# The top-1 stage of eight experts: dense over all tokens in two-part float32r, or routed by expert in places of 128 rows in plain float32

## The reference

```python
n = layernorm(h)                         # 1664 x 192
p = softmax(n @ Wg)                      # Wg: 192 x 8
e = argmax(p)                            # the token's expert
y = silu(n @ W1[e] + b1[e]) @ W2[e] + b2[e]   # 192 -> 768 -> 192
h = h + p[e] * y
```

## Time and profile before

| | |
|---|---|
| median of 3 executions | 3536.33 us (3533.74 to 3541.62) |
| profiled execution, its own time | 3540.45 us |
| its span, first to last instruction | 3538.6 us |
| mean granted TensorE clock | 0.925 of full |
| the two phases of the second layer's feed-forward | 2052.8 to 2464.9 us of the span |

### The profile page before, as it was taken

How to read it: one execution, slowest core, us unless ns; L and a number is a source line. 1 busy time by engine, 2 the same in 40 slices (tenths; PEclk the granted TensorE clock), 3 DMA queues, 4 the chain that set the end, 5 groups by cost and what they waited for, 6 DMA issues and landing times. The chain is left out here.

```text
span 3538.6 us, 61221 instructions
## 1 busy us (share of the span) xinstructions
PE 3168.4 (90%) x21505; PEld 2959.4 (84%) x21505; DVE 2348.5 (66%) x5839; ACT 1209.5 (34%) x2419; POOL 645.9 (18%) x733
## 2 busy tenths in 40 slices
PE   6769999999999999999699879999887879876687
PEld 6659999999999999999688869998676869865476
DVE  2656777777777777777486747777447657776666
ACT  2332333333333333333333333333435333234233
POOL 1111111111111111111211111111222211121220
PEclk8779999999999999999899979999998979988698
DMA  2010000000000000000000000000000010000000
GB/s 96 1 47 16 33 32 32 31 32 32 32 32 32 32 32 32 32 32 0 34 2 2 33 16 32 32 16 9 1 10 1 17 47 16 10 1 3 12 17 15
DMA packets 9707, 82.40 MB, mean 23 GB/s; under 512 B 1285, under 2 KB 1541, under 8 KB 3194
## 3 DMA queue, kind: packets, MB, share of 16 engines
q1 hardware_dynamic: 9466, 79.59, 6.1%
HBM read 78.29 MB, written 1.30 MB: 22 GB/s over the span
## 5 line engine op out<-in xcount | busy, mean ns | idle before, releaser
L716 ACT ACTIVATE hid<-bank,dat 128x384 f32<-128x384 f32 (+1 forms) x1104 | 671.7, 609 | 1404.6 <-PE bank L446 1272.6
L685 PE MATMUL bank<-w,hid_hi 128*128 128x384 f32 x3588 | 1038.2, 361 | 0.0
L687 PE MATMUL bank<-w,hid_lo 128*128 128x192 f32 x3588 | 901.8, 251 | 0.0
L687 PEld LDWEIGHTS bank<-w,hid_lo 128*128 128x128 f32 x3588 | 687.1, 191 | 1.9
L748 DVE TENSOR_TENSOR hid_lo<-hid,hid_hi 128x384 fp32r<-128x384 f32 (+1 forms) x1104 | 653.6, 592 | 38.4
L685 PEld LDWEIGHTS bank<-w,hid_hi 128*128 128x128 f32 x3588 | 674.0, 188 | 1.9
L745 DVE CAST hid_hi<-hid 128x384 fp32r<-128x384 f32 (+1 forms) x1104 | 413.0, 374 | 174.5 <-ACT hid L716 173.1
L759 DVE SCALAR_TENSOR_TENSOR h_tok<-bank,gate,h_tok 128x192 f32<-128x192 f32 x520 | 216.8, 417 | 318.6 <-PE bank L687 312.1
L446 PE MATMUL bank<-xa_hi,w_hi 128*128 128x384 f32 (+1 forms) x1104 | 402.2, 364 | 9.9 <-DVEq L1741 5.6
L446 PE MATMUL bank<-xa_hi,w_lo 128*128 128x384 f32 (+1 forms) x1104 | 394.3, 357 | 0.0
L446 PE MATMUL bank<-xa_lo,w_hi 128*128 128x384 f32 (+1 forms) x1104 | 394.1, 357 | 0.0
(11 more groups left out here) (291 smaller groups left out, 4234.1 us busy)
## 6 DMA issues: line engine op xcount, KB each, us to landing
raw<-in_L_exp SPq DMA_DIRECT2D x44, 1344.0 KB, 5.7
pix<-in_pixels SPq DMA_DIRECT2D x6, 832.0 KB, 9.1
wp_raw<-in_L_att SPq DMA_DIRECT2D x1, 2880.0 KB, 9.4
raw<-in_L_mlp SPq DMA_DIRECT2D x2, 1344.0 KB, 5.7
wp_raw<-in_L_att SPq DMA_DIRECT2D x2, 768.0 KB, 4.1
tok<-in_tok SPq DMA_DIRECT2D x1, 1248.0 KB
out<-h_tok SPq DMA_DIRECT2D x1, 1248.0 KB, 4.4
wp_raw<-in_L_fat SPq DMA_DIRECT2D x1, 960.0 KB, 4.8
```

The lines of the kernel that those rows point to most:

```text
L685: nc.tensor.matmul(o[:, 0:2 * D], hid_hi[k % 2][:, m, c], w2[j][:, m, :], start=m == 0, stop=False)
L687: ins = nc.tensor.matmul(o[:, 0:D], hid_lo[k % 2][:, m, c], w2[j][:, m, 0:D], start=False, stop=m == HC - 1)
L716: nc.scalar.activation(hid[(6 * k + m) % 3][:, 0:128 * nt], bank[4 + (6 * k + m) % 4][:, 0:128 * nt], func, bias=bias).then_inc(s["h_act"] ...
```

## The change

The two phases keep their place and are written anew. No float32r splits are left in them. `features_phase(plain=True)` evacuates the turned tokens in float32 (`x_f`) and leaves out VectorE's low parts, and no weights are split beside it. The logits are made token-major: 26 products, two for each tile, with the tile's turned tokens stationary and the 8 gate columns moving. `routed_phase` then sorts the tokens by expert: VectorE counts the chosen tokens over the tiles (`cum`), TensorE ranks them, VectorE works out a destination row for each token (`slot`) and the expert of each place (`place`). A place is 128 rows of one expert; there are always 20 of them (`PLACES`, (1664 + 8 x 127) // 128), whatever the routing. GpSimd scatters the 13 tiles of normalised tokens to a DRAM table `route_rows` by 13 indirect DMAs. Then for each place: SyncE reads the expert's number from `place`, loads that expert's weights (1,348 KB, three buffers `w_e`) and the place's 128 rows (`x_in`, four buffers); TensorE turns the rows (`turn`), VectorE copies them out of PSUM (`keep_x`), TensorE makes the six hidden chunks with two float32 products each (`up`), ScalarE applies Silu, TensorE makes the result with six products (`down`, one place later), VectorE copies it (`keep_y`) and GpSimd scatters it to a DRAM table `route_back` by token number. At the end SyncE reads the 1,664 rows back in four loads and VectorE adds them, scaled, to `h_tok`. A cleared table of 2 MB is written to `route_rows` at the start of the kernel.

```diff
+ROW = 200
+PLACES = (TOK + 8 * 127) // 128
+PACK = RAW + 8
+ROUTE_COLS_8 = 128 + 128 + 13 * 8 + 64 + PLACES * 8
...
-                        for o in ((feat[:, part, c],) if ln else ((xa_hi, xb)[part][:, c],)):
+                        for o in ((feat[:, part, c],) if ln else (x_f[:, part, c],) if plain else ((xa_hi, xb)[part][:, c],)):
...
-                for i, (t0, n) in enumerate(TBLK):
+                for i, (t0, n) in enumerate(() if plain else TBLK):
...
+                if plain:
+                    w = dat[:, DATA_COLS[g_col]].rearrange("p (k e) -> p k e", k=2)
+                    for t in range(TILES):
+                        c = slice(128 * t, 128 * t + 128)
+                        nc.tensor.matmul(bank[0][:, E * t:E * t + E], x_f[:, 0, c], w[:, 0, :], start=True, stop=False)
+                        ins = nc.tensor.matmul(bank[0][:, E * t:E * t + E], x_f[0:DB, 1, c], w[0:DB, 1, :], start=False,
+                                               stop=True)
+                    ins.then_inc(s["job_full"].sem, 1)
+                    return
...
+            def sync(sp):
+                sp.wait_ge(route["places"], 1)
+                for p in range(N):
+                    if p >= 3:
+                        sp.wait_ge(route["y_full"], p - 2)
+                    e = sp.value_load(place[0:1, p:p + 1], min_val=0, max_val=E - 1)
+                    sp.dma_start(w_e[p % 3][:, :], pack[bass.ds(e, 1)].rearrange("o p n -> p (o n)"))\
+                        .then_inc(w_e_in[p % 3], 16)
+                    if p == 0:
+                        sp.wait_ge(route["rows_out"], 16 * TILES)
+                    if p >= 4:
+                        sp.wait_ge(y_out[p % 4], 16 * (p // 4))
+                    sp.dma_start(x_in[p % 4][:, :], rows_d[128 * p:128 * p + 128, :]).then_inc(x_e_in[p % 4], 16)
+                for j in range(4):
+                    sp.wait_ge(y_out[j], 16 * (N // 4))
+                for q, (t0, nt) in enumerate(BLOCKS):
+                    sp.dma_start(y_tok[:, t0:t0 + nt, :], back_d[128 * t0:128 * (t0 + nt), :]
+                                 .rearrange("(t p) d -> p t d", p=128)).then_inc(y_tok_in[q], 16)
+
...
+            def gpsimd(pool):
+                pool.wait_ge(route["rows_clear"], 16)
+                pool.wait_ge(route["tables"], 32)
+                pool.wait_ge(route["slots"], 1)
+                for t in range(TILES):
+                    nc.gpsimd.indirect_dma_start(rows_d[:, :], bass.IndirectOffsetOnAxis(slot[:, t:t + 1], 0),
+                                                 x_ext[:, t, :], None).then_inc(route["rows_out"], 16)
+                for p in range(N):
+                    pool.wait_ge(route["y_kept"], p + 1)
+                    pool.wait_ge(x_e_in[p % 4], 16 * (p // 4 + 1))
+                    nc.gpsimd.indirect_dma_start(
+                        back_d[:, :], bass.IndirectOffsetOnAxis(x_in[p % 4][:, D:D + 1].bitcast(I32), 0),
+                        y_e[p % 4][:, :], None).then_inc(y_out[p % 4], 16)
+            def tensor(pe):
+                gating["tensor"][0](pe)
...
+                nc.tensor.matmul(bank[0][:, TILES * E:TILES * E + E], ones, last[:, TILES - 1, :], start=True, stop=True)
+                nc.tensor.matmul(o, tri, chosen, start=True, stop=False)
+                nc.tensor.matmul(o[:, E:], ones, last[:, 0:TILES - 1, :].rearrange("p t e -> p (t e)"),
+                                 start=False, stop=True).then_inc(route["ranked"], 1)
...
+                def turn(p):
+                    pe.wait_ge(x_e_in[p % 4], 16 * (p // 4 + 1))
+                    if p >= 2:
+                        pe.wait_ge(route["x_kept"], p - 1)
+                    ident = shp[:, SHAPE_COLS["ident"]]
+                    nc.tensor.transpose(bank[6 + p % 2][:, 0:128], x_in[p % 4][:, 0:DA], ident)
+                    nc.tensor.transpose(bank[6 + p % 2][0:DB, 128:256], x_in[p % 4][:, DA:D], ident)\
+                        .then_inc(route["x_turned"], 1)
+                def up(p):
+                    pe.wait_ge(w_e_in[p % 3], 16 * (p // 3 + 1))
+                    pe.wait_ge(route["x_kept"], p + 1)
+                    w = w_e[p % 3]
+                    for m in range(HC):
+                        n = HC * p + m
+                        if n >= 4:
+                            pe.wait_ge(route["hid_full"], n - 3)
+                        o = bank[n % 4][:, 0:128]
+                        nc.tensor.matmul(o, w[:, 128 * m:128 * m + 128], x_t[p % 2][:, 0:128], start=True, stop=False)
+                        nc.tensor.matmul(o, w[0:DB, HID + 128 * m:HID + 128 * m + 128], x_t[p % 2][0:DB, 128:256],
+                                         start=False, stop=True).then_inc(route["up_full"], 1)
+                def down(p):
+                    if p >= 2:
+                        pe.wait_ge(route["y_kept"], p - 1)
+                    for m in range(HC):
+                        pe.wait_ge(route["hid_full"], HC * p + m + 1)
+                        ins = nc.tensor.matmul(bank[4 + p % 2][:, 0:D], h_e[p % 2][:, m, :],
+                                               w_e[p % 3][:, 2 * HID + D * m:2 * HID + D * m + D],
+                                               start=m == 0, stop=m == HC - 1)
+                    ins.then_inc(route["y_full"], 1)
+                turn(0)
+                up(0)
+                for p in range(1, N):
+                    turn(p)
+                    up(p)
+                    down(p - 1)
+                down(N - 1)
...
+                steps = ((c3, cum[1], 1), (cum[1], cum[0], 2), (cum[0], cum[1], 4), (cum[1], cum[0], 8))
+                for f, o, w in steps:
+                    nc.vector.tensor_copy(o[:, 0:w, :], f[:, 0:w, :])
+                    link(nc.vector.tensor_tensor(o[:, w:TILES, :], f[:, w:TILES, :], f[:, 0:TILES - w, :], ALU.add))
...
+                def keep_x(p):
+                    dve.wait_ge(route["x_turned"], p + 1)
+                    if p >= 2:
+                        dve.wait_ge(route["up_full"], HC * (p - 1))
+                    nc.vector.tensor_copy(x_t[p % 2][:, 0:128], bank[6 + p % 2][:, 0:128])
+                    nc.vector.tensor_copy(x_t[p % 2][0:DB, 128:256], bank[6 + p % 2][0:DB, 128:256])\
+                        .then_inc(route["x_kept"], 1)
+                def keep_y(p):
+                    dve.wait_ge(route["y_full"], p + 1)
+                    if p >= 4:
+                        dve.wait_ge(y_out[p % 4], 16 * (p // 4))
+                    nc.vector.tensor_copy(y_e[p % 4][:, :], bank[4 + p % 2][:, 0:D]).then_inc(route["y_kept"], 1)
+                keep_x(0)
+                for p in range(1, N):
+                    keep_x(p)
+                    keep_y(p - 1)
+                keep_y(N - 1)
+                for q, (t0, nt) in enumerate(BLOCKS):
+                    dve.wait_ge(y_tok_in[q], 16)
+                    for t in range(t0, t0 + nt):
+                        nc.vector.scalar_tensor_tensor(res[:, t, :], y_tok[:, t, :], inv[:, t:t + 1], res[:, t, :],
+                                                       ALU.mult, ALU.add)
...
-        load, split, w = expert_weights(8, a["L1_exp"], ("av_full", signals["av_full"].at + 2 * 14))
-        attention(l1, h_tok, load)
-        features_phase(n_tok, split, norm_of=h_tok)
-        g = gates(8, "L1_g", None, "top1")
-        experts_phase(8, a["L1_exp"], "L1_b1", "L1_b2", h_tok, ACT.Silu, w, g)
+        attention(l1, h_tok)
+        features_phase(x_ext[:, :, 0:D], dict(sync=lambda sp, n=len(phases): sp.wait_ge(s["phase_done"].sem, 3 * n)), route_tables(), norm_of=h_tok, plain=True)
+        g = gates(8, "L1_g", None, "top1", plain=True)
+        routed_phase(a["L1_exp"], "L1_b2", h_tok, g)
...
+            sp.dma_start(route_rows, a["rows_clear"]).then_inc(route["rows_clear"], 16)
```

More of the change, by code:

```diff
@@ L191, in vit_tower @@
         at.close()
+        dp = ExitStack()
+        x_ext = sb("x_ext", [128, TILES, ROW], scope=dp)
+        x_f = sb("x_f", [128, 2, TOK], scope=dp)
+        rp = sb("rp", [128, ROUTE_COLS_8], scope=dp)
+        w_e = [sb(f"w_e{j}", [128, PACK], scope=dp) for j in range(3)]
+        x_in = [sb(f"x_in{j}", [128, ROW], scope=dp) for j in range(4)]
+        x_t = [sb(f"x_t{j}", [128, 256], scope=dp) for j in range(2)]
+        h_e = [sb(f"h_e{j}", [128, HC, 128], scope=dp) for j in range(2)]
+        y_e = [sb(f"y_e{j}", [128, D], scope=dp) for j in range(4)]
+        cum = [sb(f"cum{j}", [128, TILES, 8], scope=dp) for j in range(2)]
+        tot = sb("tot", [128, 8], scope=dp)
+        nbl = sb("nbl", [128, 3, 8], scope=dp)
+        wide = sb("wide", [128, 8 * PLACES], scope=dp)
+        slot_f = sb("slot_f", [128, TILES], scope=dp)
+        slot = sb("slot", [128, TILES], I32, dp)
+        place_f = sb("place_f", [1, PLACES], scope=dp)
+        place = sb("place", [1, PLACES], I32, dp)
+        dp.close()
         bank = [pb(f"bank{j}") for j in range(8)]
@@ L491, in exponents @@
                 NJ = TOK // 4
```

(28 more changed lines are left out.)

106 lines of the change are left out of this document (94 added, 12 removed).

## The result

The changed kernel takes **3373.06 us** (median of four runs, 3369.58 to 3377.08) against 3538.34 for the kernel before beside it: ratio 0.9534, 95% interval 0.9516 to 0.9552, 165 us less. The prediction was 208 us less, 3328; its range to 3390 holds the time, its likeliest case doesn't. The profiled execution's span is 3374.2 us.

What follows compares the result with a forecast made beforehand. It took TensorE's product work, with chains ahead, to bound the two phases. New terms 14.3 + 11.5 + 7.9 + 20.6 + 138 + 11.4 = 203.7 us replace 412.1, giving 3328 us; range 3295 to 3390.

Steps and rivals of the forecast that it cites:

- wrong if the period isn't paced by the load: Twenty places: a sign that would refute the forecast, which had a 6.7 us period paced by load and products together.
- What bounds the kernel, and the gain's direction: Replaced phases, 412.1 us: mostly TensorE's product work, with chains ahead; the change was to save 208.4 us, faster at 0.98.
- Features, 14.3: Features phase: 21.3 us falls by 7.0, without weight splits slowing two small VectorE operations and without low parts.
- Logits and gates, 11.5: Gates phase, 15.1 us before: 52 records make 8.0 us, VectorE's chain 3.3, getting into the phase 0.2.
- Sorting, 7.9: Sorting tokens by expert: VectorE's counts 2.0 us, TensorE 1.6, VectorE's chain of 13 to 14 operations 4.3.
- The end, 11.4: After the last place: `keep_y` 0.4 us, GpSimd 1.4, landing 2.4, four loads 5.5, last additions 1.7.
- Scatter, 20.6: Scatter of rows to `route_rows`: 13 indirect DMAs at 1.4 us, the geometric middle of 0.56 and 3.5, plus 2.4 landing.
- rival 4: Dear scatter: 3.5 us an issue, partly from VectorE's additions holding GpSimd up; 29 us more, 3357. Chance 0.14.
- The twenty places, 138: Loop over places: 14.1 us to the first `down`, 121.2 for 18 periods of about 6.7, last `down` 2.4.
- Up to 128 columns I use 0.112: Places: each record of `up`'s float32 products steps by 0.112 us, so its 24 records take 2.69 us.
- the phases behind are as they were: Phases after the new stage: no change of time; no term was given for them.
- Rival 3: Cold clock in the places: `up` and `down` at half clock, body 10.5 us, 76 us more, 3404. Chance 0.10.

Runs made afterwards that it cites:

- experiment 6: Changed kernel with its 64-row products kept, four weight buffers for three, ten buffers for rows and results for four: 3373.99 us, ratio 0.9539.
- Experiment 2: Changed kernel with the second logits product of each tile on all 128 rows, gate columns zero in rows 64 to 127: 3371.05 us, ratio 0.9528.
- experiment 1: Changed kernel with the second product of every hidden chunk in `up` on all 128 rows, the added rows zero: 3319.56 us, ratio 0.9373.
- experiment 7: Changed kernel with zero-filled 128-row second products in both `up` and the logits: 3317.55 us, ratio 0.9384.
- experiment 11: Changed kernel with 48 unused columns put back in table `dat`, so tiles behind it return to their old addresses: 3381.48 us, ratio 0.9552.
- experiment 3: Changed kernel with `up`'s chunks in pairs, two products of 128 rows, then the two of 64: 3347.31 us, ratio 0.9465.
- experiment 10: Rows loaded ahead of weights, on the changed kernel with 128-row products, four weight and ten row/result buffers, and `turn` between `up` and `down`: 3282.07 us, ratio 0.9275.

## Why the prediction was right or wrong, by its own steps

**The prediction's own sign**, "wrong if the period isn't paced by the load", came true: in the changed kernel TensorE's products pace every place, and the load is hidden (experiment 6). The time lies in the range, but the mechanism of the places failed.

**What bounds the kernel, and the gain's direction**: right. The dense experts were TensorE's work, and computing 20 x 128 rows for 8 x 1664 pays for everything added.

**Features, 14.3**: 13.2. The two small operations of the earlier trace rows are gone down to their short form, as the step said:

```profile
2046.46 0.17 DVE L432 TENSOR_SCALAR rstd<-mv 128x2 f32<-128x2 f32 x1
...
2047.99 0.17 DVE L432 TENSOR_SCALAR rstd<-mv 128x4 f32<-128x4 f32 x1
```

**Logits and gates, 11.5**: 14.5. The logits took 11.2 for 8.0; the row that I took (8 rows, all alike) had no change of rows in it. Experiment 2 gives 8.3.

**Sorting, 7.9**: 7.0. **The end, 11.4**: 10.7.

**Scatter, 20.6**: 18.6, from the sorted slots at 2080.3 to 2098.9, where the first place's rows are asked for; they are on the chip at 2100.9, 2.0 us that the prediction has in the places (2.4). The issue was cheaper than its term:

```profile
2082.63 0.96 POOL L869 DMA_INDIRECT route_rows<-x_ext,slot  x1 [0.30 <-issue]
2083.89 0.96 POOL L869 DMA_INDIRECT route_rows<-x_ext,slot  x1 [0.30 <-issue]
...
2090.21 0.96 POOL L869 DMA_INDIRECT route_rows<-x_ext,slot  x1 [0.30 <-issue]
2091.48 0.96 POOL L869 DMA_INDIRECT route_rows<-x_ext,slot  x1 [0.30 <-issue]
```

An issue steps by 1.26 us for the 1.4 of a geometric middle. The first begins 0.9 us behind the slots, thirteen take 16.3, and 1.4 after the last the rows are out. A geometric middle of two bounds six times apart was a guess, and that it came near was luck. The landing of these scatters, which the changed kernel's trace does not list, is 2.4 us in experiment 1's, as the term had it. The step is the same 1.26 while VectorE makes its additions (to 2086.2) and after them. So rival 4's hold did not occur.

**The twenty places, 138**: 192.3. This is the step that failed, and in it one sentence, "Up to 128 columns I use 0.112". The row is of products that all have 128 rows; `up`'s alternate. Per place at full clock that is 5.0 us for 2.69, and 8.07 for a body of 5.9. It makes the loads' 7.05 us hidden, and so the pacing that the step describes never began. Of the 54 us, (8.07 - 6.7) x 20 = 27 are this, (9.27 - 8.07) x 20 = 24 the clock, 0.83 over the places where I had chosen 0.9, and 3 remain. The cut is rough: the 6.7 already has a clock of 0.9 in it, and without that the first part is larger and the second smaller. In experiment 1, with equal rows, the clock is 0.94 (over its places) and the period 6.93. So most of the second half goes away with the first. What links them was not isolated.

The rest of the step held. `down`'s 0.178 was 0.171. The number's read costs less than the 1.0 us taken: `down(p-3)` ends near 2124.7, and the load that waits for it is issued at 2125.41. The rows are issued 0.38 us behind the weights and land 6.1 us later, so from `down(p-3)` to `turn(p)` the loads take 0.7 + 0.4 + 6.1 = 7.2 us for 7.05. The step's alternation, 6.4 and 7.1, shows in experiment 1 as 5.8 and 7.5 in the two places read there, and its period 6.7 was 6.75 in experiment 7, at a clock of 0.96 for the 0.9 taken; so near a hit has luck in it.

The Trainium skill (TensorE: Matmul & The Clock Gate, section on packing small matmuls) has the line that a weight load overlaps with a product in flight only when the row groups differ. This case's rows show the opposite of that line: next to a product on the same 128 rows the load begins 0.11 us ahead of its own product (experiment 1, 0.112 us a record), and where 128 and 64 rows alternate it begins only with it. The measurement decides.

**The sum.** The stage is 52.6 us above its term. Around it the time is 8.6 less: 7.2 ahead, nearly all of it experiment 11's addresses, and 1.4 behind. 3328 + 52.6 - 8.6 = 3372, measured 3373. The prediction had "the phases behind are as they were" and nothing on those ahead but the clearing, whose cost of nothing holds: it lands after 20.8 us, under the convolution, and the next loads are issued at 43.7 us for 44.9 before.

**The rivals.** Rival 3, the cold clock, was there in part: one place in three. (Its terms, 1.0 + 5.4 + 3.9, make a body of 10.3, not 10.5; that is 4 us in its total.) None of them, and not the range, had a longer product at full clock in it. The range held because it reached towards rival 3, for another reason: that the time lies in it is luck as far as the places go.

## What to carry to other kernels

Cost a product by a row whose neighbours are like its neighbours: a stream of like products tells nothing about a stream in which they alternate. Where a sum over 192 rows is cut in two, cut it in 96 and 96 (47 us here), fill the short part with zeros (54 us), or put products of like rows together (26 us). And when TensorE gets faster, look at the loads again: first the number of buffers, which was worth nothing under the slow products and 20 us under the fast ones, then which transfer stands first in the queue, 12 us.

## What the runs showed of the hardware

- A float32 product of two records steps by 0.223 us at full clock with 128 stationary columns, for 8 and for 128 moving columns, for 96 and 128 rows, and by the sum of experiment 3 for 64, if the product before has as many rows. A change between 128 and 64 rows adds 0.19 us at 128 moving columns and 0.093 at 8.
- With equal rows the weight load of a product of 128 moving columns begins 0.11 us ahead of it, beside the product before; where 128 and 64 rows alternate it begins with its own product (experiment 1 and the changed kernel).
- GpSimd issues an indirect DMA of 128 rows in 0.96 us, one each 1.26 us; in the places it lands after 6.3 to 6.6 us, in experiment 10 after 4.8.
- A stage that no edit touched took 6.7 us in 1260 more with its tiles 192 bytes further on.
- One core's loads moved 318 GB/s over 94 us beside a TensorE busy for 98% of them (experiment 10).
